# Destination tiles formed per bucket, and the second layer's neighbour sums begun within its projection

## The reference

```python
x = x + gnn0(layernorm(x))     # relu([x_i, x_j, edge] @ mW1 + mb1) @ mW2 + mb2, summed over the edges of src,
                               # then relu([x, sums] @ uW1 + ub1) @ uW2 + ub2, plus its input
x = x + ffn0(layernorm(x))     # shared MLP 256-256-128-256, and two of four experts 256-128-64-256, gated
x = x + sage(sage(layernorm(x)))   # two layers, relu between them
x = x + ffn1(layernorm(x))     # one score per node, half of them get a 256-1024-256 MLP

def _sage_conv(x, src, tgt, W_l, b_l, W_r):
    msgs = x[src]
    agg = jax.ops.segment_sum(msgs, tgt, num_segments=n)
    deg = jax.ops.segment_sum(jnp.ones((src.shape[0],), x.dtype), tgt, num_segments=n)
    agg = agg / jnp.maximum(deg, 1.0)[:, None]
    return agg @ W_l + b_l + x @ W_r
```

## Time and profile before

| | before |
|---|---|
| median of 3 runs | 2958.7 us (2958.1 to 2959.84) |
| the profiled execution, its own time | 2963.02 us |
| its span in the trace | 2960.8 us |
| TensorE busy | 2468.8 us (83%) |
| VectorE busy | 1909.6 us (64%) |
| POOL busy | 1809.9 us (61%) |
| ACT busy | 1019.1 us (34%) |
| sort, edges, nodes end at | 602, 1295, 1737 us |
| layer 0's neighbours, projection, layer 1's neighbours, last stage end at | 2127, 2169, 2755, 2961 us |

### The profile page before, as it was taken

One profiled execution on the slowest core, in us unless ns is written; L12 is line 12 of the kernel. 1 busy time (PEld: TensorE's weight loads), 2 busy tenths in 40 slices (PEclk: granted clock), 3 DMA queues, 4 the chain that ended last, 5 costly groups with the idle time before them and its releaser, 6 DMA issues. The chain is left out here.

```text
span 2960.8 us, 35471 instructions
## 1 busy us (share of the span) xinstructions
PE 2468.8 (83%) x8644; PEld 1444.2 (49%) x8644; DVE 1909.6 (64%) x3873; ACT 1019.1 (34%) x2851; POOL 1809.9 (61%) x1880
## 2 busy tenths in 40 slices
PE   5588997289999999989998858888777777778799
PEld 2144443045555555546666645555444444343577
DVE  8997876267777777744535656666654444444888
ACT  1277778157776777742222210000110000000232
POOL 5777777767676767630037757777547777777200
PEclk8799999589999999999999989999777777876899
DMA  9222324079999999982056665555343333333001
GB/s 281 72 84 85 96 88 160 14 218 269 263 264 266 262 263 265 266 245 74 27 167 204 201 191 168 169 169 166 94 133 106 105 105 106 106 105 105 22 1 45
DMA packets 238394, 446.46 MB, mean 151 GB/s; under 512 B 47451, under 2 KB 129005, under 8 KB 237999
## 3 DMA queue, kind: packets, MB, share of 16 engines
q0 software_dynamic: 96288, 254.83, 31.9%
q1 hardware_dynamic: 136416, 184.09, 19.0%
q10 hardware_dynamic: 5488, 5.28, 0.5%
HBM read 320.06 MB, written 126.13 MB: 151 GB/s over the span
## 5 line engine op out<-in xcount | busy, mean ns | idle before, releaser
L1780 POOL DMA_INDIRECT nbr_yg<-y_d,gidx x763 | 721.6, 946 | 245.4 <-PE nbr_sum L1890 130.7
L1890 PE MATMUL nbr_sum<-nbr_yg,nbr_hot 128*128 128x258 f32 x1526 | 603.9, 503 | 216.3 <-DMA nbr_yg<-y_d,gidx 169.9
L887 POOL DMA_INDIRECT qg<-q_d,rb x480 | 481.8, 1004 | 207.7 <-DVE hb L973 114.3
L1828 DVE TENSOR_TENSOR nbr<-nbr_sum,nbr 128x258 f32 x763 | 323.6, 424 | 435.6 <-PE nbr_sum L1890 411.4
L1890 PEld LDWEIGHTS nbr_sum<-nbr_yg,nbr_hot 128*128 128x128 f32 x1526 | 299.8, 232 | 503.6 <-DMA nbr_yg<-y_d,gidx 187.9
L413 POOL DMA_INDIRECT recs_d<-recs,slot_src x416 | 409.5, 984 | 150.3 <-issue 138.5
L1004 PE MATMUL p_sum<-hb,wide 128*96 128x512 f32 x960 | 452.1, 593 | 2.6 <-ACT hb L933 2.6
L933 ACT ACTIVATE hb<-hb 128x512 f32<-128x512 f32 x480 | 295.9, 630 | 208.8 <-DVE hb L973 207.3
L973 DVE TENSOR_TENSOR hb<-p_h,qg 128x512 f32<-128x512 f32 x480 | 310.1, 680 | 21.6 <-DMA qg<-q_d,rb 20.0
L1278 POOL DMA_INDIRECT n_ahead<-y_d,gidx x165 | 156.7, 949 | 268.2 <-DMA y_d<-n_y 200.6
L437 ACT ACTIVATE lane_hot<-bare_hot,val 128x128 f16<-128x128 f16 x832 | 247.5, 392 | 123.5 <-DVE bare_hot L671 123.5
(11 more groups left out here) (321 smaller groups left out, 3466.5 us busy)
## 6 DMA issues: line engine op xcount, KB each, us to landing
agg_d<-agg SPq DMA_DIRECT2D x240, 192.4 KB, 5.2
msg_d<-n_ahead SPq DMA_DIRECT2D x165, 128.0 KB, 2.7
nbr_ys<-msg_d SPq DMA_DIRECT2D x165, 128.0 KB, 2.5
nbr_yg<-y_d,gidx POOLq DMA_INDIRECT x763, 2.8
p_low<-p_d SPq DMA_DIRECT2D x11, 768.0 KB, 12.4
recs_d<-fill SPq DMA_DIRECT2D x16, 510.0 KB
rb<-recs_d SPq DMA_DIRECT2D x60, 136.0 KB, 4.9
qg<-q_d,rb POOLq DMA_INDIRECT x480
```

Source lines behind the costliest of these rows:

```text
L887: pool.indirect_dma_start(qg[t % QB][:, :], None, S.q[:, :], bass.IndirectOffsetOnAxis(ap=rb[n % RB][:, t % BT, 1:2].bitcast(U32), axis=0) ...
L1780: pool.indirect_dma_start(yg[n % YB][:, 0:D], None, S.y[:, :], bass.IndirectOffsetOnAxis(ap=C.gidx[:, FROM + n:FROM + n + 1], axis=0)).the ...
L1828: dve.tensor_tensor(nbr, p_sum[t % SUMS][:, 0:W], nbr, ALU.add).then_inc(s_acc, 1)
L1890: pe.matmul(p_sum[t % SUMS][:, 0:W], hot[t // BT % HOTS][:, column, :], rows[:, :], start=True, stop=True).then_inc(s_sum, 1)
```

## The change

**Sort.** Only the number of tiles and the way in which cells are laid down change. The two cells of a bucket may now share a tile: NTILE is (53125 + 25 x 127) // 128 = 439, and 440 columns. The first late rows of a bucket fill the last early tile. Counts of cells become tiles in two rounds through TensorE (`tiles_of_cells`) with small matrices that VectorE makes after the source ranks (`maps_between_cells`, twenty steps); another matmul makes a row that is added to the column numbers (`p_iota`), so that the table comes out with the columns of a bucket's late part permuted. The lane one-hot takes the constant `iota_f`; the copy at L539 goes. MIXED becomes 47, NSTORED 141.

```diff
 NCELL = 2 * NT
-NTILE = (N_EDGES + NCELL * (P - 1)) // P
+NTILE = (N_EDGES + NT * (P - 1)) // P
...
-MIXED = -(-2 * N_EDGES // (NCH * P)) // STORED_PER
+MIXED = -(-(-(-2 * N_EDGES // NCH) - NT * (P - 1)) // P) // STORED_PER
...
+                step.link(dve.tensor_scalar(pair_w[:, :, :], bucket_row[:, :, :], own_bucket[:, 0:1], None, ALU.is_equal))
+                step.link(dve.tensor_scalar(early_w[:, :, :], pair_w[:, :, :], is_early[:, 0:1], None, ALU.mult))
+                step.link(dve.tensor_scalar(tiles_w[:, :, :], bucket_row[:, :, :], own, is_early[:, 0:1], ALU.is_gt, ALU.mult))
...
+            def tiles_of_cells():
+
+                dve.tensor_copy(grp[:, :], total[:, EC - 1:EC].to_broadcast([2 * HALF, 2])).then_inc(s_grp, 1)
+                dve.wait_ge(s_start, 2)
+                step.link(dve.tensor_scalar(whole_i[:, 0:1], starts[0:2 * HALF, 0:1], P - 1.0, None, ALU.add))
+                step.link(dve.tensor_copy(whole_i[:, 1:2], starts[0:2 * HALF, 2:3]))
+                step.link(dve.tensor_scalar(first_slot[:, :], starts[0:2 * HALF, 2:3], of_late[:, 0:1], None, ALU.mult))
+                step.link(dve.tensor_scalar(whole_i[:, :], whole_i[:, :], 7, None, ALU.logical_shift_right))
+                step.link(dve.tensor_scalar(grp[:, 0:1], whole_i[:, 0:1], of_late[:, 0:1], None, ALU.mult))
+                step.link(dve.scalar_tensor_tensor(out=grp[:, 0:1], in0=whole_i[:, 1:2], scalar=sign[:, 0:1],
+                                                   in1=grp[:, 0:1], op0=ALU.mult, op1=ALU.add))
+                dve.tensor_copy(grp[:, 1:2], whole_i[:, 0:1]).then_inc(s_grp, 1)
+                dve.wait_ge(s_start, 3)
+                step.link(dve.scalar_tensor_tensor(out=first_slot[:, :], in0=starts[0:2 * HALF, 7:8], scalar=float(P),
+                                                   in1=first_slot[:, :], op0=ALU.mult, op1=ALU.add))
+                step.link(dve.tensor_copy(jumps[:, :], starts[0:HALF, 8:9].to_broadcast([HALF, P])))
...
-                step.link(dve.tensor_scalar(grp_i[:, :], total[:, EC - 1:EC], float(GRAINS[k] - 1), None, ALU.add))
-                step.link(dve.tensor_scalar(grp_i[:, :], grp_i[:, :], 8 - k, None, ALU.logical_shift_right))
-                dve.tensor_copy(grp[:, :], grp_i[:, :].to_broadcast([2 * HALF, 2])).then_inc(s_grp, 1)
-                dve.wait_ge(s_start, k + 1)
-                step.link(dve.tensor_scalar(first_slot[:, :], starts[0:2 * HALF, 0:1], float(GRAINS[k]), None, ALU.mult))
+                if k == 0:
+                    groups_of_buckets()
+                else:
+                    tiles_of_cells()
...
+                    maps_between_cells()
...
+                    step.link(dve.tensor_tensor(p_iota[:, 0:NCOL], tr[:, 0:NCOL], C.iota_h[:, :], ALU.add))
...
+                    over_cells(0, pair_w)
+                    over_cells(2, early_w).then_inc(s_start, 1)
+                    pe.wait_ge(s_grp, 3)
+                    over_cells(4, before_w)
+                    over_cells(6, tiles_w)
+                    over_cells(8, jump_w).then_inc(s_start, 1)
...
+                    last = pe.matmul(tr[:, 0:NCOL], jumps[0:nb, :], reached[0:nb, 0:NCOL], start=True, stop=True)
```

```diff
+                act.activation(of_stored[:, :, :],
+                               C.zeros_w[:, 0:W].rearrange("p (a n) -> p a n", a=1).to_broadcast([P, NT, W]),
+                               ACT.Copy).then_inc(s_nbr_zero, 1)
+                for place in range(NT):
+                    act.wait_ge(s_z, place + 1)
+                    act.activation(C.z[:, place, :], p_z[:, 0:D], ACT.Copy).then_inc(s_z_taken, 1)
...
-                    dve.memset(of_stored[:, :, :], 0.0).then_inc(s_nbr_zero, 1)
-                dve.wait_ge(s_nbr_zero, 3 - layer)
+                dve.wait_ge(s_nbr_zero, 2)
...
-                    if t >= JOIN:
+                    if JOIN <= t < JOIN + NT:
...
-                    for tile in range(NTILE - JOIN, NT):
-                        join(tile, NTILE - 1)
```

```diff
+        BT, GB, PER, HOTS, SUMS, EVERY = 8, 18, 3, 3, 6, 16
...
+        p_sum = tr.banks + out.banks
...
+        HOT_AFTER = {11: 0, 14: 1, 17: 2}
...
+                    sp.dma_start(S.y[p * P:(p + 1) * P, :], y[p % YB][:, :]).then_inc(s_yst[p % YB], 16)
...
+                for b in range(GB):
+                    pool.memset(yg[b][:, D:W], 1.0).then_inc(s_zero, 1)
+                for b in range(YB):
+                    pool.wait_ge(s_yst[b], 16 * len(range(b, EARLY_NODES // P, YB)))
+                for t in range(NTILE):
+                    if t == NSTORED:
+                        for b in range(YB):
+                            pool.wait_ge(s_yst[b], 16 * len(range(b, NT, YB)))
+                    if t >= GB:
+                        pool.wait_ge(s_sum, t - GB + 1)
+                        pool.nop(nofuse=True)
+                    pool.indirect_dma_start(yg[t % GB][:, 0:D], None, S.y[0:EARLY_NODES, :] if t < NSTORED else S.y[:, :],
+                                            bass.IndirectOffsetOnAxis(ap=C.gidx[:, t:t + 1], axis=0)
+                                            ).then_inc(s_gath[t // PER % len(s_gath)], 16)
...
+                act.wait_ge(s_h, NT)
+                act.activation(C.nbr[:, :, :], C.zeros_w[:, 0:W].rearrange("p (a n) -> p a n", a=1).to_broadcast([P, NT, W]),
+                               ACT.Copy).then_inc(s_nbr_zero, 1)
...
+                def mean(p):
+                    if p % CH == 0:
+                        dve.tensor_copy(rdeg_at[:, p // CH, :],
+                                        C.rdeg[:, :, :].rearrange("p (c a) b -> p c (a b)", a=CH)[:, bass.ds(chunks_at[p // CH], 1), :]
+                                        .rearrange("p a n -> p (a n)")).then_inc(s_deg_at, 1)
+                        dve.wait_ge(s_deg_at, p // CH + 1)
+                    if p >= HB:
+                        dve.wait_ge(s_x, p - HB + 1)
+                    nbr = (C.nbr[:, :, :].rearrange("p (c a) w -> p c a w", a=CH)[:, bass.ds(chunks_at[p // CH], 1), p % CH, 0:D]
+                           .rearrange("p a d -> p (a d)"))
+                    dve.scalar_tensor_tensor(out=h[p % HB][:, :], in0=nbr, scalar=rdeg_at[:, p // CH, p % CH:p % CH + 1],
+                                             in1=C.z[:, p, :], op0=ALU.mult, op1=ALU.add).then_inc(s_h, 1)
...
+                chunks_at = load_own_buckets(nc, dve, C.chunk_at[:, 0:NCH], NCH - 1)
+                dve.tensor_scalar(C.rdeg[:, :, :], C.nbr[:, :, D:D + 1], 1.0, None, ALU.max).then_inc(s_deg, 1)
+                dve.wait_ge(s_deg, 1)
+                dve.reciprocal(C.rdeg[:, :, :], C.rdeg[:, :, :]).then_inc(s_deg, 1)
+                dve.wait_ge(s_deg, 2)
+                for p in range(MEANS):
+                    mean(p)
+                dve.tensor_copy(p_iota[:, 0, :], C.iota_f[:, :]).then_inc(s_iota, 1)
+                dve.wait_ge(s_iota, 1)
+                for p in range(NT):
+                    product(p)
+                    if p + MEANS < NT:
+                        mean(p + MEANS)
+                    if p in HOT_AFTER:
+                        one_hot(HOT_AFTER[p])
+                dve.wait_ge(s_nbr_zero, 1)
+                for t in range(NTILE):
+                    if t % BT == 0:
+                        buckets = load_own_buckets(nc, dve, C.bucket[0:1, 1, t:t + BT], NT - 1)
+                    accumulate(t, buckets[t % BT])
...
+                pe.wait_ge(s_zero, GB)
+                for t in range(NTILE):
+                    place, at = divmod(t, EVERY)
+                    if at % (EVERY // KD) == EVERY // KD - 1 and place < NT:
+                        product(place, at // (EVERY // KD))
+                    if t % BT == 0:
+                        pe.wait_ge(s_hot, t // BT + 1)
+                    if t == len(tr.banks):
+                        pe.wait_ge(out.empty, NT)
+                    if t >= SUMS and t % 2 == 0:
+                        pe.wait_ge(s_acc, t - SUMS + 2)
+                    if t % PER == 0:
+                        b = t // PER % len(s_gath)
+                        pe.wait_ge(s_gath[b], C.gathered[b] + 16 * (PER * (t // GB) + min(PER, NTILE - t)))
+                    pe.matmul(p_sum[t % SUMS][:, 0:W], hot[t // BT % HOTS][:, t % BT, :], yg[t % GB][:, :], start=True,
+                              stop=True).then_inc(s_sum, 1)
```

More of the change, by code:

```diff
@@ L248, in sorting_programs @@
         free_row = found[0:1, :, :].rearrange("p a n -> p (a n)")
-        still, late, cell = free_row[:, 0:NGS], free_row[:, 0:NTILE], reached[0:1, 0:NTILE]
+        still, late, cell = free_row[:, 0:NGS], free_row[:, 0:NCOL], reached[0:1, 0:NCOL]
         stats = m.sb("stats", [P, CH, 6])
@@ L716, in sort_tensor @@
                 pe.wait_ge(s_reached, k + 1)
-                pe.matmul(starts[:, 2:2 + ng], C.ones[0:nb, :], reached[0:nb, 0:ng], start=True,
-                          stop=True).then_inc(s_bkt, 1)
```

(27 more changed lines are left out.)

291 lines of the change are left out of this document (173 added, 118 removed).

## The result

| | before | after |
|---|---|---|
| median | 2959.27 us (2958.1 to 2967.01, 4 runs) | 2926.74 us (2918.62 to 2930.14, 4 runs) |
| ratio to before | | 0.9879, interval 0.9862 to 0.9897 |
| profiled span | 2960.8 us | 2926.1 us |

The kernel is 32.5 us faster. 68.5 were forecast, and the time lies above the range of 2877 to 2915.

A forecast was written before the change was run, and what follows sets the result against it. POOL's gathers, 1.25 us each, were taken to bound the layers, its scatters the sort's end. 31.3 + 18.9 + 2.05 + 8.8 + 9.0 - 1.5 = 68.5 us off gave a median of 2890.2, range 2877 to 2915.

The forecast's parts named there:

- Net 1.5 us on: Sort: added VectorE steps delay the ranks, scatter 28 stalls 2.2 us, a removed copy saves 0.65; net 1.5 us longer.
- just enough: Sort, scatter 76: its cover of 7.0 us ahead of the first table group shrinks to about 1, so no stall.
- rival four: Layer 1's start: ten means after the tenth store block POOL for their length, 4.3 us; 2895 us, chance 0.05.
- Layer 1, fewer tiles and the stall: Layer 1's gathers: 464 become 439 at 1.25 us each, 31.3 us off; one stall of 2.05 us goes too.
- Earlier start: Layer 1: POOL waits only for the tenth stored tile of y, so the first gather comes 18.9 us sooner.
- Layer 0: Layer 0: one direct gather fewer 1.25, clearing moved to ACT 6.7, joins moved inside the loop 0.8; 8.8 us off.
- Node stage: Node stage: with fewer gathers ahead, the last y store ends it instead; 9.0 us off, bounds 0 and 11.
- Eighteen buffers: Layer 1's start: POOL gathers 18 tiles, 22.5 us, before it needs a sum, so it does not stall.
- Rival 3: Sort: covers fail, POOL waits at scatters 28 and 76, 9 us instead of 1.5; 2898 us, chance 0.05.
- Rival 1: Layer 1's early start fails, POOL held until the projection is over; price 18.9 us, 2909 us, chance 0.12.
- Rival 2: Node stage does not get shorter, as pacing or remaining stores end as late; 2899 us, chance 0.08.
- Rival 5: Layer 1: TensorE becomes the bound at a lower clock, 1.47 us per tile; slower, 3002 us, chance 0.03.

The follow-up runs named there:

- e6: The changed kernel with the lane numbers of the table's one-hots read from PSUM again instead of SBUF; 2899.2 us, ratio to before 0.9767.
- e5: The changed kernel as it is, measured again as the standard of its series; 2932.2 us, ratio to before 0.9879.
- e18: The kernel of e6, but POOL waits for all 25 tiles of y before layer 1's first gather; 2912.4 us, ratio to before 0.9832.
- e8: The kernel before, with the one-hots' lane numbers read from the SBUF constant instead of PSUM; 2972.1 us, ratio to before 1.0020.
- e7: The changed kernel with its table 464 columns wide instead of 440, lane numbers still in SBUF; 2901.8 us, ratio to before 0.9797.
- e17: The changed kernel with its table 448 columns wide instead of 440, lane numbers still in SBUF; 2912.7 us, ratio to before 0.9836.
- e11: The kernel of e6 with 12 gather buffers in pairs instead of 18 in threes; ratio to before 0.9727, in a series where all kernels ran slower.

## Why the prediction was wrong

- **Sort**: the step that failed is "Net 1.5 us on"; 37.8 were measured. It counted the steps before the ranks and left out what the diff does to the 52 lane one-hots: it moves an input from PSUM to SBUF. Their duration doesn't change, so they were given no price. They cost 33 us (e6 against e5), by hits on scatters in the stretch that POOL ends. Without the holds the last scatter is at 602.6, 5.8 us later than before, not 1.5. The stall at scatter 28 came as forecast, 2.3 us beyond the usual 0.30 (2.2 forecast); but at scatter 76, where the cover was called "just enough", e6 stalls for another 2.55. Scatter 28 in the trace after, scatter 76 in e6's:

```profile
85.70 0.97 POOL L419 DMA_INDIRECT recs_d<-recs,slot_src  x1 [2.64 <-DVE found L654]
```

```profile
150.78 0.97 POOL L420 DMA_INDIRECT recs_d<-recs,slot_src  x1 [2.85 <-PE acc L801]
```

- **The rule that was weighed at the wrong place**: rival four took the Trainium skill, "SBUF — State Buffer", section "SBUF: two separate sides", for the ten means beside the first gathers. In my words: while VectorE works on two SBUF inputs, a POOL instruction that reads SBUF is kept out, and the other way round. Beside the gathers the trace agrees, but it bites little: the mean at 2181.28 held the gather at 2181.44 for 0.18 us, and no other. The prediction said that the accumulates beside the gathers don't test the rule, and looked no further. Another place of the same trace did test it. VectorE and POOL in the trace before, where VectorE adds two SBUF tiles in the sort:

```profile
173.91 1.49 DVE L655 TENSOR_TENSOR xc<-xc,xnc 128x1280 f32<-128x1280 f32 x1
175.44 1.49 DVE L657 TENSOR_TENSOR xc<-xc,u2b 128x1280 f32<-128x1280 f32 x1
```

```profile
174.72 1.52 POOL L413 DMA_INDIRECT recs_d<-recs,slot_src  x1 [0.31 <-issue]
176.55 1.22 POOL L413 DMA_INDIRECT recs_d<-recs,slot_src  x1 [0.30 <-issue]
```

  The left-over of the add less 0.13 gives 0.55 and 0.25, and the scatters are just that much above 0.97. With it the price of the new one-hots could have been bounded between 0 and 52 x 1.09 = 57 us.
- **Layer 1, fewer tiles and the stall**: right, 33.1 of 33.3 us.
- **Earlier start**: right, 17.2 of 19.7 us with the joins (e18 against e6: 19); VectorE's first step of the stage came after 4.53 us of idling instead of 2.70.
- **Layer 0**: right, 7.9 of 8.0 us.
- **Node stage**: the mechanism is right, and that its size came out is in part luck. 8.7 of 9.0 us hold between the marks of the table, but layer 0's start is better counted from the last edge gather: 450.1 us before and 439.2 after. In the other undisturbed traces it is 452.7 with the nodes of before (e8), and 435.9 to 438.9 with those of the change (e5 to e7, e17, e18). So the term is 11 to 17 us; where the part above 9 comes from stays open.
- **Eighteen buffers**: right. The first accumulate came 21.8 us after the first gather (2190.74 against 2168.93), 21.6 were forecast, and no gather waited for it. The clearing on ACT took 5.57 us; 6.4 were forecast, though the step from 0.39 to 0.63 us gives 6.2. That no gather waited shows the cover, not that twelve buffers would have been too few (e11).
- Rivals 1, 2 and 5 did not happen. Rival 4 happened once, 0.18 us of its 4.3. Rival 3 had the right place and sign, a sort that eats up the gain. Its own mechanism, waits at scatters 28 and 76, gave some 5 us in e6; the loss of 37.8 is four times its 9 and came by another.

The kernel of e6 beats both: 2899.2 us, 67.6 below before in its series. With the one-hots' input back in PSUM the forecast sum of 68.5 is nearly reached, in part by luck: the sort is 5.8 us longer instead of 1.5 and layer 1's start gives 17.0 us instead of 19.7, while the node stage gives more than forecast.
